# Running each token tile's load, first LayerNorm and transposes inside its own iteration in an eight-core S4 and LoRA kernel

## The chip, the cores and the metric

The kernel runs on all 8 cores of one Trainium2 chip. Each core takes 1024 of the 8192 tokens and computes its rows of the output alone; weights are read by every core. The metric is device time in microseconds (us) of the slowest core. Five engines work side by side on a core, each through its own list in order: PE (TensorE, matmuls and transposes), DVE (VectorE), ACT (ScalarE), POOL (GpSimd, here only to issue transfers) and SP (SyncE, which issues the other transfers).

## The reference, cut to what matters

```python
x = L0_attn_u                                   # (1, 8192, 4096) float32
x = x + _layernorm(_L0_attn_ref(_layernorm(x), ...))   # causal long convolution + D*u
x = x + _layernorm(_L0_ffn_ref(_layernorm(x), ...))    # x @ kernel + bias + LoRA terms

# _L0_attn_ref, along the last axis (L = 4096):
K = _s4_kernel(Lambda, p, q, B, Ct, step, L)
y = irfft(rfft(u, n=2*L) * rfft(K, n=2*L), n=2*L)[..., :L]
return y + D[0] * u

# _L0_ffn_ref, one LoRA choice per 1024 tokens:
base_out = x @ kernel + bias
Ax = einsum('bri,bti->btr', A_eff, x);  delta = einsum('bor,btr->bto', B_eff, Ax)
delta += einsum('or,btr->bto', lora_B_shared, einsum('ri,bti->btr', lora_A_shared, x))
return base_out + delta

# _layernorm(x): (x - mean) / sqrt(var + 1e-5), along the last axis
```

## The kernel before, in words

A core's 1024 tokens are 8 tiles of 128 tokens by 4096 features. The program has four stages. First a setup stage builds the convolution kernel as a banded matrix (`tband`) and the LoRA matrices. Then comes the tile loop, which the change touches: for every tile the first LayerNorm, the convolution, the second LayerNorm with its residual, the third LayerNorm and the transposed copy that the last matmuls need. Then the matmuls with the 4096 by 4096 weights run in 8 column blocks (L901), and at last the rows are read back, normalised and added (L951 to L972).

The order on each engine is the order in which the Python code emits instructions; there is no scheduler. Every instruction of DVE and ACT also waits for the one before it on its engine (L41). The work of one tile is in five functions:

- `emit_load_ln1` (L698): SP issues the load of the tile, 2 MB, into `xb[t % 2]` (L706). It waits until the tile two earlier, which held that buffer, has been stored and normalised. DVE sums the tile (L709) while ACT sums its squares (L713); DVE and ACT turn the sums into mean and scale in a chain of tiny operations (`ln_finalize`, L662 to L674); ACT writes the normalised tile in bf16 (L723) into `n1b` or `n1c`, which take turns.
- `emit_convtransp` (L726): PE transposes the 32 blocks of that tile into two PSUM buffers `ptrb` (L738), eight at a time; DVE copies each eight to `xfmt` (L742). There is one `xfmt`.
- `emit_conv` (L748): 8 groups of 4, 8, ..., 32 matmuls against `tband` (L763, 144 in all). Groups take turns on three PSUM buffers `pconv`, so the fourth group waits for the copy of the first. DVE adds `D` times the input as it copies a group out to `ya` (L770), ACT sums the squares (L775).
- `emit_post1` (L781): the second LayerNorm's statistics, the residual sum `x1` into `xb` (DVE, L794), its store to memory (SP, L798), and the third LayerNorm: sum (DVE, L801), squares (ACT, L806), small chain, normalised tile (ACT, L811) into the same bf16 buffer.
- `emit_post2` (L814): four rounds of eight transposes (PE, L823), a copy to `n2fm` (DVE, L827) and eight small matmuls with the LoRA matrix (PE, L834).

Before, the load and first LayerNorm of the next tile are emitted ahead of the convolution of the present one, and the next tile's transposes between `emit_post1` and `emit_post2` of the present one. After the last tile, DVE copies `pax` out (L855), and the column blocks start (L889).

Of the kernel before, what the change touches and what calls it, by code (L numbers as in the profile page):

```python
# [135 lines left out]
def build_nc(t_tiles=8):  # L136
    nc = bass.Bass("TRN2", target_bir_lowering=False)
    TT = t_tiles
# [37 lines left out]
    with ExitStack() as ctx:  # L176
# [482 lines left out]
        def ln_finalize(st, n_elems, t_s1tok, t_q1tok, a_guard=None):  # L659
            guards = [st.get("_ra"), a_guard]  # L660
            W("vector", [t_s1tok, t_q1tok] + [g for g in guards if g is not None])
            a = E("vector", lambda v: v.tensor_scalar(out=st["mean"][:, :], in0=st["s1"][:, :], scalar1=1.0 / n_elems, scalar2=None, op0=OP.mult))  # L662
            b = E("vector", lambda v: v.tensor_scalar(out=st["var"][:, :], in0=st["q1"][:, :], scalar1=1.0 / n_elems, scalar2=EPS, op0=OP.mult, op1=OP.add))
            W("vector", [a, b])
            c = E("vector", lambda v: v.tensor_scalar(out=st["rstd"][:, :], in0=st["mean"][:, :], scalar1=st["mean"][:, :], scalar2=-1.0, op0=OP.mult, op1=OP.mult))
            W("vector", [c])
            d = E("vector", lambda v: v.tensor_tensor(out=st["var"][:, :], in0=st["var"][:, :], in1=st["rstd"][:, :], op=OP.add))
            W("vector", [d])
            f = E("vector", lambda v: v.reciprocal(out=st["rstd"][:, :], in_=st["var"][:, :]))
            W("scalar", [f])  # L670
            g = E("scalar", lambda s: s.activation(out=st["rstd"][:, :], in_=st["rstd"][:, :], func=AF.Sqrt))
            st["_ra"] = g
            W("vector", [g])
            h = E("vector", lambda v: v.tensor_scalar(out=st["nbias"][:, :], in0=st["mean"][:, :], scalar1=st["rstd"][:, :], scalar2=-1.0, op0=OP.mult, op1=OP.mult))  # L674
            return g, h
# [22 lines left out]
        def emit_load_ln1(t_i):  # L698
            xbt = xb[t_i % 2]
            st = st1p[t_i % 2]  # L700
            nb = n1bufs[t_i % 2]
            war = [t_x1store[t_i - 2], t_n2_tok[t_i - 2], t_rs2_tok[t_i - 2]] if t_i >= 2 else (
                [t_ksum_done, t_bacc, t_bbcast] + xb0_guard if t_i == 0
                else [t_rdim, prev_ev] + xb1_guard + [t_ksum_done])
            W("sync", war)
            t_uload[t_i] = DMA("sync", f"uin{t_i % 2}", lambda s, t_i=t_i, xbt=xbt: s.dma_start(  # L706
                out=xbt[:, :], in_=u[P * t_i:P * t_i + P, :]))
            W("vector", [t_uload[t_i]] + (trv_guard if t_i == 0 else []))
            t_rs = E("vector", lambda v, xbt=xbt, st=st: v.tensor_scalar(  # L709
                out=trv[:, :], in0=xbt[:, :], scalar1=1.0, scalar2=None, op0=OP.mult, op1=OP.add,  # L710
                accum_out=st["s1"][:, :]))
            W("scalar", [t_uload[t_i]] + (tra_guard if t_i == 0 else []))
            t_sq = E("scalar", lambda s, xbt=xbt, st=st: s.activation(  # L713
                out=tra[:, :], in_=xbt[:, :], func=AF.Square, accum_out=st["q1"][:, :]))
            t_r1, t_nb1 = ln_finalize(st, D, t_rs, t_sq,
                                      a_guard=t_n1_tok[t_i - 2] if t_i >= 2 else None)
            toks = [t_nb1]
            if t_i >= 2:
                toks += [t_n2tr[t_i - 2], conv_ev_last[t_i - 2]]
            if t_i == 0:  # L720
                toks += [t_ldbs] + n1b_guard
            W("scalar", toks)
            t_n1_tok[t_i] = E("scalar", lambda s, xbt=xbt, st=st, nb=nb: s.activation(  # L723
                out=nb[:, :], in_=xbt[:, :], func=AF.Identity, bias=st["nbias"][:, :], scale=st["rstd"][:, :]))

        def emit_convtransp(t_i):  # L726
            nb = n1bufs[t_i % 2]
            evs = []
            for r in range(4):
                b = r % 2  # L730
                toks = [t_n1_tok[t_i], ptrb_last[b]]
                if t_i == 0 and r < 2:
                    toks += [t_astk, t_kmbT] + xfmt_guard
                W("tensor", toks)
                tlast = None
                for j in range(8):
                    c = 8 * r + j
                    tlast = E("tensor", lambda t, c=c, r=r, j=j, nb=nb: t.transpose(  # L738
                        out=ptrb[r % 2][:, 128 * j:128 * j + 128], in_=nb[:, 128 * c:128 * c + 128],
                        identity=idsb[:, :]))  # L740
                W("vector", [tlast] + (xfmt_guard if t_i == 0 and r == 0 else []))
                ev = E("vector", lambda v, r=r: v.tensor_copy(  # L742
                    out=xfmt[:, 1024 * r:1024 * r + 1024], in_=ptrb[r % 2][:, :]))
                ptrb_last[b] = ev
                evs.append(ev)
            ctr_ev[t_i] = evs

        def emit_conv(t_i):  # L748
            nb = n1bufs[t_i % 2]
            conv_ev = [None] * 8  # L750
            for g in range(8):
                toks = [ctr_ev[t_i][3], t_tband]
                if g >= 3:
                    toks.append(conv_ev[g - 3])
                elif t_i > 0:
                    toks.append(conv_ev_last[t_i - 1])
                else:
                    toks += [t_ksum_done, gb_toks[-1]]
                W("tensor", toks)
                tg = None  # L760
                for ij in range(4 * g + 4):
                    j0 = 512 * g - 128 * ij + 384
                    tg = E("tensor", lambda t, g=g, ij=ij, j0=j0: t.matmul(  # L763
                        out=pconv[g % 3][:, :], lhsT=xfmt[:, 128 * ij:128 * ij + 128],
                        rhs=tband[:, j0:j0 + 512], start=(ij == 0), stop=(ij == 4 * g + 3)))
                gw = []
                if g == 0:
                    gw = ([sqa_tok[t_i - 1]] if t_i >= 1 else []) + (ya_guard if t_i == 0 else [])
                W("vector", [tg] + gw)
                conv_ev[g] = E("vector", lambda v, g=g, nb=nb: v.scalar_tensor_tensor(  # L770
                    out=ya[:, 512 * g:512 * g + 512], in0=nb[:, 512 * g:512 * g + 512],
                    scalar=dbc[:, :], op0=OP.mult, in1=pconv[g % 3][:, :], op1=OP.add,
                    accum_out=yacols[:, g:g + 1]))
                W("scalar", [conv_ev[g]])
                E("scalar", lambda s, g=g: s.activation(  # L775
                    out=tra[:, 512 * g:512 * g + 512], in_=ya[:, 512 * g:512 * g + 512],
                    func=AF.Square, accum_out=yaqcols[:, g:g + 1]))
            conv_ev_last[t_i] = conv_ev[7]
            sqa_tok[t_i] = pr.now("scalar")
# [57 lines left out]
                        start=(c == 0), stop=(c == FC - 1)))  # L837
            t_n2tr[t_i] = last

        emit_load_ln1(0)  # L840
        emit_convtransp(0)
        for t_i in range(TT):
            if t_i + 1 < TT:
                emit_load_ln1(t_i + 1)
            emit_conv(t_i)
            emit_post1(t_i)
            if t_i + 1 < TT:
                emit_convtransp(t_i + 1)
            emit_post2(t_i)
        last_axmm = t_n2tr[TT - 1]  # L850
        last_convevac = conv_ev_last[TT - 1]
# [32 lines left out]
        for oc in range(8):  # L884
# [21 lines left out]
            for t2 in range(TT):  # L906
# [21 lines left out]
                if oc == 7:  # L928
                    t_i = t2
# [97 lines left out]
```

How the kernel before makes its waits and increments, by code:

```python
    def emit(self, en, fn):  # L37
        sem = self.esem[en]
        if en in ("vector", "scalar") and self.en_cnt[en] > 0:
            v = self.en_cnt[en]
            self.ops[en].append(lambda e, sem=sem, v=v: e.wait_ge(sem, v))
        self.en_cnt[en] += 1
        def wrapped(e, fn=fn, sem=sem):
            fn(e).then_inc(sem, 1)
        self.ops[en].append(wrapped)
        return (sem, self.en_cnt[en])
# [11 lines left out]
        def wrapped(e, fn=fn, sem=sem):  # L59
            fn(e).then_inc(sem, 16)
# [3 lines left out]
    def waits(self, en, toks):  # L64
        best = {}
        for t in toks:
            if t is None:
                continue
            sem, v = t
            k = id(sem)
            if k not in best or best[k][1] < v:
                best[k] = (sem, v)
        for sem, v in best.values():
            self.ops[en].append(lambda e, sem=sem, v=v: e.wait_ge(sem, v))
```

## Time and profile before

| | before |
|---|---|
| time, median of 3 runs | 1881.57 us (1880.63 to 1884.97) |
| the profiled execution, its own time | 1881.86 us |
| its span (slowest core, core 7) | 1880.3 us |
| spans of the eight cores | 1859.3 to 1880.3 us |
| busy PE / DVE / ACT / POOL | 938.4 / 438.6 / 309.7 / 167.4 us |
| tile loop, first convolution matmul to the end of the last tile | about 369 to 900 us |
| column blocks | about 901 to 1483 us |

Busy times are sums over the span, so they don't say what a stage waits for. In the tile loop each engine must be looked at inside one tile: which one works while the others wait, and what each waits for. All rows shown are of core 7. "Busy" of PE counts matmuls that overlap one another; how fast PE goes is read from the distance between starts.

### The profile page before, as it was taken

The page shows a single profiled execution, that of the slowest core. Times are in us where ns is not written, and L with a number is a line of the kernel's source. Part 1 is how long each engine was busy: PE and PEld are TensorE (multiplying, and loading weights), DVE is VectorE, ACT ScalarE, POOL GpSimd, SP SyncE. Part 2 cuts the span into 40 slices and gives each one's busy share as a digit, 9 for nine tenths or more (in the row PEclk, how much of TensorE's full clock was granted, in tenths as well). Part 3 has the DMA queues.
Part 4 walks back from the last instruction along what each step waited for, and adds up shares of the span by engine and source line. Part 5 has one row for each costly group of instructions (what it writes and reads, how often), then busy time and mean ns, then how long its engine had stood idle before and what let it go on. Part 6 is the DMA issues. An engine that isn't in the chain of part 4 may idle for free.

```text
span 1880.3 us, 13850 instructions; the slowest of 8 cores (1859.3 to 1880.3 us)
## 1 busy us (share of the span) xinstructions
PE 938.4 (50%) x4229; PEld 419.0 (22%) x4229; DVE 438.6 (23%) x826; ACT 309.7 (16%) x434; POOL 167.4 (9%) x313
## 2 busy tenths in 40 slices
PE   5350000268557756855889999999996000000000
PEld 1000000134333333432334334333433000000000
DVE  1232632343544454343010110011010111111111
ACT  2400000232323423322010110011010111111111
POOL 0002011000000000000123222222221000000000
PEclk9999999988678768867789899989988555555555
DMA  0001645311220221111556565556554333433433
GB/s 7 1 7 34 103 62 99 103 45 46 90 90 1 90 90 45 45 45 45 126 101 76 101 104 75 103 102 111 70 100 75 120 89 118 127 118 117 127 91 90
DMA packets 82715, 149.86 MB, mean 80 GB/s; under 512 B 18519, under 2 KB 51848, under 8 KB 78752
## 3 DMA queue, kind: packets, MB, share of 16 engines
q0 software_dynamic: 41248, 45.82, 18.7%
q1 hardware_dynamic: 41394, 103.15, 16.4%
q8 instruction: 35, 0.57, 0.1%
q14 instruction: 38, 0.31, 0.1%
HBM read 137.08 MB, written 52.23 MB: 101 GB/s over the span
## 4 chain that ended last, share of the span: by engine, by line
PE 45%; DMA 23%; DVE 15%; issue 6%; ACT 6%; SPq 2%; DVEq 1%; POOL 1%; ACTq 0%; POOLq 0%
PE pffn L901 24%; PE pconv L763 13%; DMA p3b<-f_scr 11%; DMA f_scr<-fstage 4%; ACT p3b L954 3%; DVE ya L964 3%; DVE xb L794 2%; DVE trv L801 2%; PE ptrb L823 2%; DMA trv<-lora_a 2%; PE pax L834 2%; DMA n1b<-lora_b 2%; DVE n2fm L827 1%; DMA wbuf<-wk 1%; SPq L968 1%
## 5 line engine op out<-in xcount | busy, mean ns | idle before, releaser
L901 PE MATMUL pffn<-wbuf,n2fm 128*128 128x512 bf16 x2048 | 463.9, 391 | 8.0 <-DMA wbuf<-wk 8.0
L763 PE MATMUL pconv<-tband,xfmt 128*128 128x512 bf16 x1152 | 264.6, 393 | 2.7 <-DVE ya L770 1.6
L901 PEld LDWEIGHTS pffn<-wbuf,n2fm 128*128 128x128 bf16 x2048 | 204.1, 100 | 267.8 <-issue 40.5
L896 POOL DMA_DIRECT2D wbuf<-wk x256 | 135.2, 529 | 965.7 <-PE pffn L901 955.9
L918 DVE TENSOR_SCALAR_CACHE_REDUCE fstage<-pffn 128x512 f32<-128x512 f32 x64 | 44.3, 691 | 502.1 <-PE pffn L907 485.7
L763 PEld LDWEIGHTS pconv<-tband,xfmt 128*128 128x128 bf16 x1152 | 115.1, 101 | 149.8 <-issue 24.9
L964 DVE SCALAR_TENSOR_TENSOR ya<-xb,nall,p3b 128x512 f32<-128x512 f32 x64 | 48.1, 751 | 352.2 <-ACT p3b L954 352.2
L922 ACT ACTIVATE tra<-fstage 128x512 bf16<-128x512 f32 x64 | 40.3, 629 | 528.2 <-DVE fstage L918 524.3
L954 ACT ACTIVATE p3b<-p3b,stf_nbias,stf_rstd 128x512 f32<-128x512 f32 x64 | 52.0, 813 | 343.5 <-DMA p3b<-f_scr 343.5
L738 PE MATMUL ptrb<-idsb,n1b 128*128 128x128 bf16 x128 | 12.5, 276 | 170.3 <-ACT n1b L723 118.8
L775 ACT ACTIVATE tra<-ya 128x512 bf16<-128x512 f32 x64 | 40.3, 629 | 176.5 <-DVE ya L770 173.7
L738 PEld LDWEIGHTS ptrb<-idsb,n1b 128*128 128x128 bf16 x128 | 11.0, 125 | 171.9 <-issue 171.1
L834 PE MATMUL pax<-n2fm,astkT 128*64 128x128 bf16 x256 | 33.0, 310 | 32.4 <-DVE n2fm L827 32.4
L713 ACT ACTIVATE tra<-xb 128x4096 bf16<-128x4096 f32 x8 | 28.9, 3617 | 110.0 <-DMA xb<-u 110.0
L770 DVE SCALAR_TENSOR_TENSOR ya<-n1c,dbc,pconv 128x512 f32<-128x512 bf16 x32 | 23.9, 747 | 95.8 <-PE pconv L763 76.4
L738 PE MATMUL ptrb<-idsb,n1c 128*128 128x128 bf16 x128 | 11.7, 264 | 67.2 <-DVE xfmt L742 67.2
L770 DVE SCALAR_TENSOR_TENSOR ya<-n1b,dbc,pconv 128x512 f32<-128x512 bf16 x32 | 23.9, 747 | 88.5 <-PE pconv L763 62.8
L889 PE MATMUL pffn<-bhl,ones2bs 2*128 2x512 bf16 x64 | 30.5, 498 | 26.9 <-DVE fstage L918 25.2
L709 DVE TENSOR_SCALAR_CACHE_REDUCE trv<-xb 128x4096 bf16<-128x4096 f32 x8 | 35.4, 4420 | 19.8 <-DMA xb<-u 19.0
L827 DVE COPY n2fm<-ptrb 128x1024 bf16<-128x1024 bf16 x32 | 22.1, 691 | 72.5 <-PE ptrb L823 72.5
L595 PE MATMUL ptrb<-idsb,trv 64*128 64x64 bf16 x32 | 2.3, 233 | 68.1 <-ACT trv L583 65.5
L806 ACT ACTIVATE tra<-xb 128x4096 bf16<-128x4096 f32 x8 | 28.9, 3617 | 43.9 <-DVE xb L794 43.9
(232 smaller groups left out, 636.9 us busy)
## 6 DMA issues: line engine op xcount, KB each, us to landing
wbuf<-wk POOLq DMA_DIRECT2D x256, 128.0 KB, 3.4
xb<-u SPq DMA_DIRECT2D x8, 2048.0 KB, 8.6
x_scr<-xb SPq DMA_DIRECT2D x8, 2048.0 KB, 6.3
xb<-x_scr SPq DMA_DIRECT2D x8, 2048.0 KB, 8.9
f_scr<-fstage SPq DMA_DIRECT2D x64, 256.0 KB, 2.7
p3b<-f_scr SPq DMA_DIRECT2D x64, 256.0 KB, 3.2
y<-ya SPq DMA_DIRECT2D x64, 256.0 KB, 2.3
n1b<-lora_b POOLq DMA_DIRECT2D x16, 256.0 KB, 4.2
```

What stands on the lines that cost most here:

```text
L763: tg = E("tensor", lambda t, g=g, ij=ij, j0=j0: t.matmul(out=pconv[g % 3][:, :], lhsT=xfmt[:, 128 * ij:128 * ij + 128], rhs=tband[:, j0:j0 ...
L770: conv_ev[g] = E("vector", lambda v, g=g, nb=nb: v.scalar_tensor_tensor(out=ya[:, 512 * g:512 * g + 512], in0=nb[:, 512 * g:512 * g + 512] ...
L775: E("scalar", lambda s, g=g: s.activation(out=tra[:, 512 * g:512 * g + 512], in_=ya[:, 512 * g:512 * g + 512], func=AF.Square, accum_out=y ...
L794: t_x1 = E("vector", lambda v, xbt=xbt: v.scalar_tensor_tensor(out=xbt[:, :], in0=ya[:, :], scalar=sta["rstd"][:, :], op0=OP.mult, in1=xbt ...
L827: t_ev2 = E("vector", lambda v, r=r, t_i=t_i: v.tensor_copy(out=bass.AP(n2fm, TOK * 8 * r + P * t_i, [[FC * TOK, P], [TOK, 8], [1, P]]), i ...
L834: last = E("tensor", lambda t, c=c, t_i=t_i: t.matmul(out=pax[:, P * t_i:P * t_i + P], lhsT=astkT[:, NS * c:NS * c + NS], rhs=bass.AP(n2fm ...
L896: t_wload[kg] = DMA("gpsimd", f"wload{kg % 4}", lambda g, f=f, oc=oc, kg=kg: g.dma_start(out=wbuf[kg % 4][:, :], in_=wk[128 * f:128 * f + ...
L901: tlast = E("tensor", lambda t, f=f, t2=t2, kg=kg: t.matmul(out=pffn[t2][:, :], lhsT=bass.AP(n2fm, TOK * f + P * t2, [[FC * TOK, P], [1, P]]),
L918: t_fev[(oc, t2)] = E("vector", lambda v, t2=t2, oc=oc, sbuf_i=sbuf_i: v.tensor_scalar(out=fstage[sbuf_i][:, :], in0=pffn[t2][:, :], scala ...
L922: t_fsq[idx] = E("scalar", lambda s, sbuf_i=sbuf_i, t2=t2, oc=oc: s.activation(out=tra[:, 512 * sbuf_i:512 * sbuf_i + 512], in_=fstage[sbu ...
L954: t_lnf = E("scalar", lambda s, fbuf=fbuf: s.activation(out=fbuf[:, :], in_=fbuf[:, :], func=AF.Identity, bias=stf["nbias"][:, :], scale=s ...
L964: p3_stt[i3] = E("vector", lambda v, t_i=t_i, pc=pc, fbuf=fbuf: v.scalar_tensor_tensor(out=ya[:, 512 * pc:512 * pc + 512], in0=xb[t_i % 2] ...
```

## The change

The prologue (load, LayerNorm and transposes of tile 0) goes, and so do the two guarded calls for tile `t_i + 1`. The loop calls all five functions for its own tile, in order. The functions themselves are the same, and so are the buffers: two `xb`, two bf16 tiles, one `xfmt`.

```diff
-        emit_load_ln1(0)
-        emit_convtransp(0)
         for t_i in range(TT):
-            if t_i + 1 < TT:
-                emit_load_ln1(t_i + 1)
+            emit_load_ln1(t_i)
+            emit_convtransp(t_i)
             emit_conv(t_i)
             emit_post1(t_i)
-            if t_i + 1 < TT:
-                emit_convtransp(t_i + 1)
             emit_post2(t_i)
```

On PE, from the first tile's transposes (`n1b`) to the second tile's convolution. Before:

```order
L738 MATMUL ptrb<-idsb,n1b 128x128 x32
L763 MATMUL pconv<-tband,xfmt 128x512 x144
L738 MATMUL ptrb<-idsb,n1c 128x128 x32
L823 MATMUL ptrb<-idsb,n1b 128x128 x8
L834 MATMUL pax<-n2fm,astkT 64x128 x8
```

Now, from the first tile's last round to the second tile's first:

```order
L823 MATMUL ptrb<-idsb,n1b 128x128 x8
L834 MATMUL pax<-n2fm,astkT 64x128 x8
L738 MATMUL ptrb<-idsb,n1c 128x128 x32
L763 MATMUL pconv<-tband,xfmt 128x512 x144
L823 MATMUL ptrb<-idsb,n1c 128x128 x8
```

The 32 transposes of the second tile (`n1c`) moved from in front of the four rounds of the first tile to behind them.

On DVE, from the third LayerNorm's last small operation of the first tile to the second tile's convolution. Before:

```order
L674 TENSOR_SCALAR st_nbias<-st_mean,st_rstd 128x1
L742 COPY xfmt<-ptrb 128x1024 x4
L827 COPY n2fm<-ptrb 128x8x128 x4
L709 TENSOR_SCALAR trv,st_s<-xb 128x4096
L662 TENSOR_SCALAR st_mean<-st_s 128x1
L663 TENSOR_SCALAR st_var<-st_q 128x1
L665 TENSOR_SCALAR st_rstd<-st_mean 128x1
L667 TENSOR_TENSOR st_var<-st_var,st_rstd 128x1
L669 RECIPROCAL st_rstd<-st_var 128x1
L674 TENSOR_SCALAR st_nbias<-st_mean,st_rstd 128x1
L770 SCALAR_TENSOR_TENSOR ya,yacols<-n1c,dbc,pconv 128x512 x8
```

Now:

```order
L827 COPY n2fm<-ptrb 128x8x128 [waits tok_tensor,tok_vector] x4
L709 TENSOR_SCALAR trv,st1b_s<-xb 128x4096 [waits dma_uin1,tok_vector]
L662 TENSOR_SCALAR st1b_mean<-st1b_s 128x1 [waits tok_vector,tok_scalar]
L663 TENSOR_SCALAR st1b_var<-st1b_q 128x1 [waits tok_vector]
L665 TENSOR_SCALAR st1b_rstd<-st1b_mean 128x1 [waits tok_vector]
L667 TENSOR_TENSOR st1b_var<-st1b_var,st1b_rstd 128x1 [waits tok_vector]
L669 RECIPROCAL st1b_rstd<-st1b_var 128x1 [waits tok_vector]
L674 TENSOR_SCALAR st1b_nbias<-st1b_mean,st1b_rstd 128x1 [waits tok_scalar,tok_vector]
L742 COPY xfmt<-ptrb 128x1024 [waits tok_tensor,tok_vector] x4
L770 SCALAR_TENSOR_TENSOR ya,yacols<-n1c,dbc,pconv 128x512 [waits tok_tensor,tok_scalar,tok_vector]
```

In both, a LayerNorm's sum and small chain (L709 to L674) stand between the copies of the last rounds and the second tile's convolution; before it is the third tile's, now the second tile's own. The four copies to `xfmt` moved behind it.

On SP, the first transfers of the loop, before (-) and now (+):

```order
 L657 DMA bhl<-bias_scr 2x4096
-L706 DMA xb<-u 128x4096 x2
+L706 DMA xb<-u 128x4096
 L798 DMA x_scr<-xb 128x4096
 L706 DMA xb<-u 128x4096
```

The second tile's load moved from right behind the first tile's load to right behind the store of the first tile's `x1`; every later load moves one tile back in the same way.

## Rows read from the trace of the kernel before

**Rows 1.** Windows (busy and count by engine, PE's granted clock, transfers): whole stages
```profile
core 7: us, PE busy (x) PEld busy (x) DVE busy (x) ACT busy (x) POOL busy (x), PEclk, DMA share, GB/s
567.00:633.00 66.00, 43.58 (x240) 23.13 (x240) 28.44 (x52) 21.28 (x26) 0.00 (x0) 0.76 0.16 64
900.00:1483.00 583.00, 508.07 (x2176) 215.80 (x2176) 47.22 (x132) 47.07 (x122) 133.00 (x252) 0.90 0.58 96
```
**Rows 2.** Windows, the same columns: inside the third and fourth tiles
```profile
501.40:535.00 33.60, 33.60 (x148) 14.80 (x148) 9.73 (x22) 9.36 (x18) 0.00 (x0) 0.93 0.00 1
535.00:555.80 20.80, 2.79 (x33) 2.35 (x31) 15.04 (x26) 8.64 (x7) 0.00 (x0) 0.63 0.24 101
555.80:567.90 12.10, 8.03 (x65) 6.42 (x66) 3.80 (x5) 3.51 (x1) 0.00 (x0) 0.50 0.44 173
```
**Rows 3.** Timeline (start, length, engine, line, idle before), end of the third tile
```profile
544.63 0.33 SPq L798 DMA_DIRECT2D x_scr<-xb  x1
551.78 3.80 ACT L811 ACTIVATE n1b<-xb,st_nbias,st_rstd 128x4096 bf16<-128x4096 f32 x1 [0.54 <-DVE st_nbias L674]
...
555.70 0.33 SPq L706 DMA_DIRECT2D xb<-u  x1
555.83 1.01 PE L823 MATMUL ptrb<-idsb,n1b 128*128 128x128 bf16 x8 [1.39 <-ACT n1b L811]
...
564.39 3.62 ACT L713 ACTIVATE tra<-xb 128x4096 bf16<-128x4096 f32 x1 [8.81 <-DMA xb<-u]
566.05 0.69 DVE L827 COPY n2fm<-ptrb 128x1024 bf16<-128x1024 bf16 x1 [2.32 <-PE ptrb L823]
566.86 4.42 DVE L709 TENSOR_SCALAR_CACHE_REDUCE trv<-xb 128x4096 bf16<-128x4096 f32 x1
567.85 32.96 PE L763 MATMUL pconv<-tband,xfmt 128*128 128x512 bf16 x144
571.54 0.15 DVE L662 TENSOR_SCALAR st_mean<-st_s 128x1 f32<-128x1 f32 x1 [0.24 <-DVE trv L709]
573.95 3.80 ACT L723 ACTIVATE n1b<-xb,st_nbias,st_rstd 128x4096 bf16<-128x4096 f32 x1 [0.59 <-PE pconv L763]
```
**Rows 4.** Timeline, first tile: from the loads to the convolution
```profile
335.37 1.14 SPq L706 DMA_DIRECT2D xb<-u  x2
351.08 4.42 DVE L709 TENSOR_SCALAR_CACHE_REDUCE trv<-xb 128x4096 bf16<-128x4096 f32 x1 [18.96 <-DMA xb<-u]
357.36 1.28 ACT L671 ACT_TABLE_LOAD   x1 [2.64 <-DVE st_rstd L669]
359.50 3.80 ACT L723 ACTIVATE n1b<-xb,st_nbias,st_rstd 128x4096 bf16<-128x4096 f32 x1 [0.65 <-DVE st_nbias L674]
363.55 1.87 PE L738 MATMUL ptrb<-idsb,n1b 128*128 128x128 bf16 x16 [118.77 <-ACT n1b L723]
368.98 7.39 PE L763 MATMUL pconv<-tband,xfmt 128*128 128x512 bf16 x24 [1.12 <-DVE xfmt L742]
```
**Rows 5.** Line L706 (loads), times to landing: the first two, then the other six
```profile
DMA to landing us min/median/max: 15.4/17.6/19.8
...
DMA to landing us min/median/max: 8.4/8.6/8.7
```
**Rows 6.** Lines L798 (stores of x1), then L896 (weights, the first four), times to landing
```profile
DMA to landing us min/median/max: 6.3/6.3/7.2
...
DMA to landing us min/median/max: 6.4/7.7/16.2
```
**Rows 7.** Waits of the tile loop: who, for whom, us, times, longest
```profile
PE pconv L763 <- DVE ya L770: 1.6, 4, 0.6
```
**Rows 8.** Timeline of PE's weight loads, one for each matmul: start of two convolutions
```profile
506.02 0.15 PEld L763 LDWEIGHTS pconv<-tband,xfmt 128*128 128x128 bf16 x1 [0.28 <-issue]
506.38 28.16 PEld L763 LDWEIGHTS pconv<-tband,xfmt 128*128 128x128 bf16 x131 [0.20 <-issue]
...
633.99 0.13 PEld L763 LDWEIGHTS pconv<-tband,xfmt 128*128 128x128 bf16 x2 [0.17 <-issue]
636.06 3.77 PEld L763 LDWEIGHTS pconv<-tband,xfmt 128*128 128x128 bf16 x18 [0.23 <-issue]
```

## The prediction
> **What bounds the kernel now.** I read the windows first, to see which stage the change touches. A tile takes 66 us of the loop and the column blocks behind it take 583 us [rows 1]; the change touches neither a matmul there nor a transfer of theirs, so I take those blocks and the last stage as shifted, not changed. Next the windows inside one tile [rows 2]: a convolution of 33.6 us in which PE is busy throughout; then 20.8 us in which PE has 2.8 us of work and DVE 15.0 (the post stage: statistics, `x1`, third LayerNorm); then 12.1 us of alternation of PE and DVE. That sum, 66.5, is the tile's period: the tile is a serial chain of convolution, LayerNorms and rounds. What the reader is to see is that the next tile's LayerNorm stands *beside* this chain, under the convolution.
>
> Then the timeline of one tile's end [rows 3]. The last copy of the rounds starts at 566.05, DVE goes to the sum of a following tile at 566.86, and PE starts the next convolution at 567.85, without waiting for that sum: its input was normalised and transposed before. The normalising pass of the tile prepared there runs at 573.95, when PE is six us into its convolution.
>
> **What the change puts on the chain.** After it, the convolution of tile t+1 needs the sum L709, the small chain, L723, 32 transposes and four copies, all emitted behind the rounds of tile t. Up to the last copy of the rounds nothing in front changes: the third LayerNorm's result ends at 551.78 + 3.80 = 555.58 and the first round starts at 555.83 [rows 3], and the `xfmt` copies that go from there ran beside L811, so their going gives nothing.
>
> From the sum's start the new chain is, in steady rows [rows 3]: L709 at 566.86 to L723 at 573.95, 7.09 us; L723 itself 3.80. Its last part was never on the chain later than tile 0, but there it was [rows 4]: L723 ends at 363.30, the transposes start at 363.55, and the convolution at 368.98, so 0.25 + 5.43 = 5.68 us. Sum 7.09 + 3.80 + 5.68 = 16.57. Tile 0 gives the same in one piece: 351.08 to 368.98 is 17.90, less its single table load of 1.28, 16.62 [rows 4]. Before, the same stretch (L709's start to the convolution's start) took 567.85 - 566.86 = 0.99 [rows 3]. So each of the 7 passages from a tile to the next costs 16.6 - 1.0 = **15.6 us, together 109.2**. Bounds for one passage: 15.0, if the transposes (1.87 us for 16 in rows 4) took half as long and only the copies counted; 17, if half a us of waiting came at each of three handovers.
>
> What lies beside other work: the load. SP now issues it right behind the store of `x1`: 544.63 + 0.33 = 544.96 on this time base, where before it waited until 555.70, since the buffer of the tile just finished had to be free [rows 3]. It is wanted at 566.86 by DVE, 21.9 us later. Alone a load lands in 8.4 to 8.7 us [rows 5] and a store in 6.3 [rows 6]; now they run together. The nearest rows for that are the two loads at 335.37, together 4 MB, which landed after 15.4 and 19.8 us [rows 5]. Even 19.8 is hidden. ACT's squares (3.62) come after landing and are wanted at 571.54: 544.96 + 19.8 + 3.62 = 568.4, hidden too. Cost 0; what is late next is DVE, which gets to L709 only after the four copies. Nothing else is queued behind the load on SP before the next store, a tile later. Without the cover, each us past 566.86 costs one us a tile.
>
> **What it gives back.** (1) DVE no longer has another tile's sum and chain in front of the first convolution copy. PE waited for these copies 1.6 us in the whole loop, 4 times [rows 7]; rounding up for waits that hide in the groups, -1.8. Bounds 0 and -4. (2) The first load no longer shares with the second. It landed in 15.4; alone the others take 8.6 [rows 5], but the first four weight loads run beside it and took 6.4 to 16.2 [rows 6]. So it lands in 8.6 to 15.4; I take 11, between, since the second load is the greater part of the other traffic: -4.5, bounds 0 and -6.8. The chain at that place is load, L709 and on [rows 4], so it counts in full.
>
> **The clock.** The matmuls at the start of every convolution are 0.43 us apart and later ones 0.22; the clock in the rounds ahead was 0.50, the 1.2 GHz level, and 0.93 over a convolution [rows 2]. The slow part lasted 5.0 us in the longest case (501.35 to 506.38) and 2.1 in the shortest (633.99 to 636.06) [rows 8]; half of its length is lost time. After the change PE has only transposes in the 10 us ahead of a convolution, as at tile 0. I add 0 for it. Bounds: each of 7 starts as the longest instead of the mean of the two, (5.0 - 3.55) / 2 x 7 = +5; each as the shortest, -5.
> The Trainium skill, "TensorE: Matmul & The Clock Gate", Part 4 (PE-mode transpose), says that transposes don't count as PE activity to the clock gate. Then every convolution would start as cold as the longest rows, and the sum would be 5 us higher; rows 2 can't tell, since real matmuls (L834) are mixed with transposes there and the clock is low all the same.
>
> **Sum.** 109.2 - 1.8 - 4.5 = +102.9. The profiled execution took 1881.86, so 1984.8; it lies 0.3 above the median of the runs, which leaves **1984.5 us**. Bounds together: passages 105 to 119, give-backs -10.8 to 0, clock -5 to +5. The ends don't meet all at once; 1972 to 1998 is the forecast's own range, with some us for the column blocks, whose weight loads meet other cores' traffic.
>
> **Rivals.**
>
> *The load comes too late.* Store and load in one queue, on all cores in step, might serialise worse than two loads. If the load took 19.8 only after the store's 6.3, it would land at 571.1, 4.2 late: 7 x 4.2 = +29, 2014. For it: the store is new beside the load. Against: the rows of two loads together have the same 4 MB and land inside the gap. Chance 0.04.
>
> *The load is exposed whole.* If the loop behaved as one without double buffering (the load starting when the tile's last work ends), 7 x 8.6 = +60 on top, 2045. The two `xb` are still there and SP's waits for tile t+1 are on tile t-1, so only a queue held by something unseen would do it. Chance 0.01. The Trainium skill, "Trainium Kernel Development and Optimization", Best Practices, tells to double-buffer so that DMA overlaps compute; read as a rule against this change it gives this case, yet what is given up here by the rows is the overlap of DVE, ACT and PE, not that of the load.
>
> *The clock stays down longer.* If all 24 matmuls of the first three groups ran at 0.43, a convolution would have 24 x 0.43 = 10.3 us of slow part instead of 3.55, 3.4 us lost, times 7 = +24, 2008. For it: PE idles longer ahead of a convolution. Against: at tile 0 PE had idled 118.77 us [rows 4] and its 24 matmuls took 7.39, not 10.3. Chance 0.04.
>
> *Not slower.* DVE has gaps of 2.32 us in each of four rounds (9.3 us) and ACT 8.81 [rows 3]. If the next tile's sum and chain ran in them and the transposes under L723, the passage would cost nothing and the give-backs stay: 1881.6 - 6.3 = 1875. It decides from the point where L709 starts before the first round's copy, near 557, which asks for 10 us sooner. Against: DVE takes its list in order, L709 stands behind the last L827, and L723 can't be read by PE before it ends. Chance 0.01.
>
> **How the numbers follow.** Forecast 0.90, the others 0.04, 0.01, 0.04, 0.01. About 0.2% (4 us) is what a measurement of this kernel can tell from no change. Faster has only the last rival, 0.01; within 0.2% is a sliver of the same kind, 0.01; slower 0.98. The range 1972 to 1998 leaves out the rivals (0.10) and some 0.08 of the forecast's tails.
>
> **What would show it.** In the profile after: periods of a tile near 82 us instead of 66; L709 directly behind the fourth L827, with no wait for the load; PE idle about 11 us between the last L834 and the first L738 and again in pieces to the convolution; the convolution itself 33 to 34 us as before, without waits for L770; `xb<-u` landing between 9 and 20 us, before DVE asks; the column blocks near 580 us. DVE idle before L709 with "DMA xb<-u" as its releaser would make the load the step that failed; a convolution of 36 us or more the clock; a column stage that differs by over 8 us would mean that I was wrong to take it as shifted.

## The result and the profile after

| | before | after |
|---|---|---|
| median | 1880.32 us (10 runs) | 1985.43 us (10 runs) |
| ratio after to before | | 1.0549, 95% interval 1.053 to 1.0568 |
| profiled execution, its span | 1881.86, 1880.3 us | 1985.44, 1983.1 us |
| first to last convolution start, the eight cores | 463.6 to 466.3 us | 566.6 to 568.9 us |

The plain medians are 105 us apart; the ratio, 1.0549, makes the cost 103 us. 1984.5 us, 102.9 more than before, had been predicted. A few executions of every kernel here are some per cent longer at a lower clock on one die; ratios leave them out, plain medians don't. Nearly all of the difference lies in the tile loop, which grew by 103.1 us on average over the cores. The slowest core of the profiled execution is now core 1; the rows of after are of that core. The lines behind the loop have moved up by four in the changed file (L901 is L897).

The windows of one tile, with the columns of [rows 1] (time, busy of each engine, PE's granted clock, transfers), answer to [rows 2]:

```profile
core 1: us, PE busy (x) PEld busy (x) DVE busy (x) ACT busy (x) POOL busy (x), PEclk, DMA share, GB/s
608.70:642.20 33.50, 33.50 (x144) 14.53 (x144) 5.29 (x14) 5.06 (x14) 0.00 (x0) 0.93 0.00 1
642.20:663.30 21.10, 0.03 (x1) 0.01 (x1) 12.28 (x22) 8.64 (x7) 0.00 (x0) 0.63 0.51 195
663.30:675.40 12.10, 8.03 (x64) 6.37 (x64) 3.45 (x5) 3.71 (x2) 0.00 (x0) 0.50 0.02 9
675.40:690.70 15.30, 3.75 (x33) 3.18 (x32) 7.57 (x12) 4.00 (x2) 0.00 (x0) 0.50 0.00 0
```

The first three stages are as long as before. A fourth one of 15.3 us is new, in which one engine at a time works. Where DVE had 9.73 us of work under the convolution it now has 5.29: what was hidden there came out. The timeline of the same tile's end (start, length, engine, line, idle before) answers to [rows 3, 4]:

```profile
652.11 0.33 SPq L798 DMA_DIRECT2D x_scr<-xb  x1
652.63 0.33 SPq L706 DMA_DIRECT2D xb<-u  x1
659.26 3.80 ACT L811 ACTIVATE n1c<-xb,st_nbias,st_rstd 128x4096 bf16<-128x4096 f32 x1 [0.54 <-DVE st_nbias L674]
664.95 3.62 ACT L713 ACTIVATE tra<-xb 128x4096 bf16<-128x4096 f32 x1 [1.89 <-DMA xb<-u]
673.55 0.69 DVE L827 COPY n2fm<-ptrb 128x1024 bf16<-128x1024 bf16 x1 [2.32 <-PE ptrb L823]
674.71 4.42 DVE L709 TENSOR_SCALAR_CACHE_REDUCE trv<-xb 128x4096 bf16<-128x4096 f32 x1 [0.47 <-DVE n2fm L827]
681.80 3.80 ACT L723 ACTIVATE n1b<-xb,st_nbias,st_rstd 128x4096 bf16<-128x4096 f32 x1 [0.59 <-DVE st_nbias L674]
685.85 1.87 PE L738 MATMUL ptrb<-idsb,n1b 128*128 128x128 bf16 x16 [10.43 <-ACT n1b L723]
690.76 10.59 PE L763 MATMUL pconv<-tband,xfmt 128*128 128x512 bf16 x38 [1.01 <-DVE xfmt L742]
```

DVE reaches L709 behind the last L827, and what ended its short idle was its own copy, not the load, whose data ACT had squared from 664.95 to 668.57. From that copy's start (673.55) to the convolution's (690.76) are 17.2 us; before, 1.80 (566.05 to 567.85, [rows 3]). Times to landing of the seven later loads, of the stores of `x1`, and of the first load:

```profile
DMA to landing us min/median/max: 11.8/12.2/14.5
...
DMA to landing us min/median/max: 6.3/7.1/9.2
...
DMA to landing us min/median/max: 13.7/13.7/13.7
```

In the waits of the loop the row of [rows 7], PE for L770, is gone. The rest of PE's waits ahead of a convolution is for the copies of the transposes:

```profile
PE pconv L763 <- DVE xfmt L742: 8.4, 8, 1.2
```

### The profile page after: what moved, and what is told of

It reads as the page before. It is cut to its first block, busy times and chain, and to the rows that moved or that the text cites. A ratio compares the mean times of both kernels' runs of the same rounds, so it can differ in the third digit from the quotient of the medians.

```text
span 1983.1 us, 13850 instructions; the slowest of 8 cores (1966.1 to 1983.1 us)
## 1 busy us (share of the span) xinstructions
PE 945.0 (48%) x4229; PEld 423.5 (21%) x4229; DVE 438.9 (22%) x826; ACT 309.7 (16%) x434; POOL 167.4 (8%) x313
## 4 chain that ended last, share of the span: by engine, by line
PE 44%; DMA 22%; DVE 16%; ACT 8%; issue 6%; SPq 2%; DVEq 1%; POOL 1%; ACTq 0%; POOLq 0%
PE pffn L897 23%; PE pconv L763 13%; DMA p3b<-f_scr 11%; DMA f_scr<-fstage 4%; ACT p3b L950 3%; DVE ya L960 2%; DVE xb L794 2%; DVE trv L801 2%; DVE trv L709 2%; PE ptrb L823 2%; DMA trv<-lora_a 2%; DMA n1b<-lora_b 1%; PE pax L834 1%; DVE n2fm L827 1%; PE ptrb L738 1%
## 5 line engine op out<-in xcount | busy, mean ns | idle before, releaser
L897 PE MATMUL pffn<-wbuf,n2fm 128*128 128x512 bf16 x2048 | 463.3, 390 | 4.9 <-DMA wbuf<-wk 4.9
L897 PEld LDWEIGHTS pffn<-wbuf,n2fm 128*128 128x128 bf16 x2048 | 204.1, 100 | 264.1 <-issue 36.8
L738 PE MATMUL ptrb<-idsb,n1b 128*128 128x128 bf16 x128 | 14.9, 309 | 147.4 <-ACT n1b L723 146.4
L823 PE MATMUL ptrb<-idsb,n1c 128*128 128x128 bf16 x128 | 16.5, 310 | 83.7 <-ACT n1c L811 83.7
L823 PE MATMUL ptrb<-idsb,n1b 128*128 128x128 bf16 x128 | 16.5, 310 | 83.6 <-ACT n1b L811 83.6
L770 DVE SCALAR_TENSOR_TENSOR ya<-n1b,dbc,pconv 128x512 f32<-128x512 bf16 x32 | 23.9, 747 | 113.1 <-PE pconv L763 113.1
L770 DVE SCALAR_TENSOR_TENSOR ya<-n1c,dbc,pconv 128x512 f32<-128x512 bf16 x32 | 23.9, 747 | 111.6 <-PE pconv L763 111.6
L738 PEld LDWEIGHTS ptrb<-idsb,n1b 128*128 128x128 bf16 x128 | 12.8, 142 | 149.4 <-issue 149.2
L827 DVE COPY n2fm<-ptrb 128x1024 bf16<-128x1024 bf16 x32 | 22.1, 692 | 99.2 <-PE ptrb L823 99.2
L885 PE MATMUL pffn<-bhl,ones2bs 2*128 2x512 bf16 x64 | 30.9, 505 | 26.3 <-DVE fstage L914 24.6
L713 ACT ACTIVATE tra<-xb 128x4096 bf16<-128x4096 f32 x8 | 28.9, 3617 | 72.7 <-DMA xb<-u 72.7
L709 DVE TENSOR_SCALAR_CACHE_REDUCE trv<-xb 128x4096 bf16<-128x4096 f32 x8 | 35.4, 4420 | 18.4 <-DMA xb<-u 17.2
L794 DVE SCALAR_TENSOR_TENSOR xb<-ya,sta_rstd,xb 128x4096 f32<-128x4096 f32 x8 | 35.9, 4484 | 0.8
```

Of the source, the lines that this page charges most:

```text
L794: t_x1 = E("vector", lambda v, xbt=xbt: v.scalar_tensor_tensor(out=xbt[:, :], in0=ya[:, :], scalar=sta["rstd"][:, :], op0=OP.mult, in1=xbt ...
L897: tlast = E("tensor", lambda t, f=f, t2=t2, kg=kg: t.matmul(out=pffn[t2][:, :], lhsT=bass.AP(n2fm, TOK * f + P * t2, [[FC * TOK, P], [1, P]]),
```

## The experiments

Theory: between a tile's last copy to `n2fm` and the next convolution stands a serial chain, each part costs what it measures, and the load is hidden. Rivals: the load, the clock, another engine. "Loop" is the time from the first to the last convolution start over the eight cores of the profiled execution: 464.6 us on average before, 567.7 after. All edits are to the changed kernel unless said. Where the load is split off, `emit_ln1` is `emit_load_ln1` without its L706.

**Transposes alone behind the rounds.**

```diff
+        emit_load_ln1(0)
         for t_i in range(TT):
-            emit_load_ln1(t_i)
             emit_convtransp(t_i)
+            if t_i + 1 < TT:
+                emit_load_ln1(t_i + 1)
             emit_conv(t_i)
```

> Only the 32 transposes and their copies stand behind the rounds of the tile ahead; load and LayerNorm of the next tile stay ahead of the convolution, as before. Theory (what counts is the serial chain between a tile's last copy to n2fm and the next convolution, and each part costs what it measures): the transposes start as soon as the last small matmul is done, so the passage is 1.8 + 4.9 = 6.7 us instead of 1.8, 7 times 5 = +35 on 1880, about 1915. Rival (only the LayerNorm makes the cost, the transposes hide): within 5 us of 1880. Rival (any prefetch that is broken costs the whole): about 1985.

1923.69 us, ratio 1.0232 (1.0204 to 1.0259). Loop 505 to 511, +42 where 35 was expected. The passage is right: 6.7 us from the last copy's start to the convolution in the trace. Neither rival holds. The other us a tile are a wait of PE for L770 that I had not priced here: 9.8 to 16.2 us in the loop by core, where the kernel before had 1.6 to 3.7. A timeline of core 0:

```profile
502.85 4.42 DVE L709 TENSOR_SCALAR_CACHE_REDUCE trv<-xb 128x4096 bf16<-128x4096 f32 x1
503.09 5.12 PE L763 MATMUL pconv<-tband,xfmt 128*128 128x512 bf16 x23 [1.23 <-DVE xfmt L742]
509.84 0.75 DVE L770 SCALAR_TENSOR_TENSOR ya<-n1b,dbc,pconv 128x512 f32<-128x512 bf16 x1
510.74 24.55 PE L763 MATMUL pconv<-tband,xfmt 128*128 128x512 bf16 x111 [2.53 <-DVE ya L770]
```

Here DVE starts the following tile's sum as the convolution starts, PE comes to it at full speed, fills its three buffers and waits 2.53 us. In the kernel before, the sum started a us ahead and every convolution started slowly, so this wait was only 1.6 us in all on core 7 [rows 3, 7].

**The load alone early.**

```diff
+        emit_load(0)
         for t_i in range(TT):
-            emit_load_ln1(t_i)
+            if t_i + 1 < TT:
+                emit_load(t_i + 1)
+            emit_ln1(t_i)
```

> The changed kernel, with the load of the next tile alone issued ahead of the convolution again (LayerNorm and transposes stay in their own iteration). Theory (the load was hidden in the changed kernel as well): no gain; the first load shares with the second again, so +1 to +3, 1985 to 1989. Rival (the late load or its company with the store holds DVE or ACT): 10 to 40 us faster than 1985.

Median 1990.93, ratio 1.0554 (1.0525 to 1.0584), beside 1.0549 for the changed kernel; loop 564.4 to 569.4. Giving the load all its time back gains nothing.

**A second store ahead of the load.**

```diff
+            DMA("sync", "x1out", lambda s, t_i=t_i, xbt=xbt: s.dma_start(
+                out=f_scr[P * t_i:P * t_i + P, :], in_=xbt[:, :]))
             t_x1store[t_i] = DMA("sync", "x1out", lambda s, t_i=t_i, xbt=xbt: s.dma_start(
```

> The changed kernel, with a second store of the same 2 MB in front of the store of x1 and so ahead of the next load. It measures the slack of the load. Theory: landing moves from 12.2 us after its issue to about 18.5, DVE wants it about 22 after: hidden, 1984 to 1989. Rival (the load was already near its limit): each us beyond costs 7 us, 2005 or more.

1985.14, ratio 1.0525 (1.0453 to 1.0596), loop 566.7 to 569.2. The loads land later, and nothing moves:

```profile
DMA to landing us min/median/max: 16.8/17.1/18.5
```

So some 5 us of slack at least were there. The load is out as a cause, from both sides.

**The sum cut to 8 columns.**

```diff
             t_rs = E("vector", lambda v, xbt=xbt, st=st: v.tensor_scalar(
-                out=trv[:, :], in0=xbt[:, :], ...
+                out=trv[:, 0:8], in0=xbt[:, 0:8], ...
```

> The changed kernel, with the first LayerNorm's sum taken over 8 of the 4096 columns (the rest of the sum is left out). Theory: DVE's sum of 4.42 us is on the chain in all 7 passages and becomes about 0.16; ACT's squares end long before, so 7 x 4.26 = -30, and about 1 us at the first tile, where the squares of 3.62 take over: about 1954. Rival (ACT's squares or the load are late next): the gain is cut to below 15, 1970 or more.

1942.36, ratio 1.0323 (1.0297 to 1.0349): 43 us gained, 31 expected; loop 526 to 533, 39 less. The chain shrank as expected: from L709 to L723 2.83 to 3.2 us instead of 7.1 to 7.5, 30 in 7 passages. Most of the rest is the clock: seven convolutions together took 9 us less on average over the cores. Windows around the transposes and the convolution's start, core 1, with PE's rows of the same stretch:

```profile
582.00:585.20 3.20, 0.04 (x1) 0.07 (x2) 0.00 (x0) 2.91 (x1) 0.00 (x0) 0.50 0.00 0
585.20:590.00 4.80, 3.58 (x32) 3.11 (x33) 2.77 (x4) 0.00 (x0) 0.00 (x0) 0.64 0.00 0
590.00:594.00 4.00, 3.99 (x19) 1.86 (x20) 1.51 (x4) 0.88 (x3) 0.00 (x0) 1.00 0.01 4
```

```profile
585.16 1.86 PE L738 MATMUL ptrb<-idsb,n1c 128*128 128x128 bf16 x16 [6.17 <-ACT n1c L723]
587.19 1.75 PE L738 MATMUL ptrb<-idsb,n1c 128*128 128x128 bf16 x16 [0.16 <-DVE xfmt L742]
```

The clock rose inside the transposes, and the convolution ran at the full 2.4 GHz from its first matmul. On this core all eight took 31.4 us, measured from the first matmul's start to the last L770's; in the changed kernel most took 33.4 to 33.7.

**PE kept busy in the gap: matmuls, then transposes.**

```diff
             emit_load_ln1(t_i)
+            for k in range(32):
+                if t_i > 0:
+                    E("tensor", lambda t: t.matmul(
+                        out=putil[:, :], lhsT=xfmt[:, 0:128], rhs=tband[:, 0:512],
+                        start=True, stop=True))
             emit_convtransp(t_i)
```

> The changed kernel, with 32 matmuls of 512 columns whose result nobody reads added on PE in the gap of 10.4 us between a tile's last small matmul and the next transposes. They take about 8.6 us (8 at 0.43, 24 at 0.216). Theory: the clock is low there because PE idles, and each convolution loses some 2 us to it; with the clock up, the convolution takes 31.4 instead of 33.5 and the transposes with copies 4 to 4.9: -14 to -21, 1964 to 1971. Rival (the clock's start is not set by what PE does in the gap, or it falls again before the convolution): 1985. Rival (the added work delays the transposes): slower than 1985.

1968.44, ratio 1.0455 (1.0419 to 1.0492), loop 552 to 555: 14 us less. Most convolutions took 31.4 us, transposes and copies 4.03 instead of 4.90. More work on PE made the kernel faster. The second form puts 80 transposes there instead (`ptrb[0]` from `tband`, after a wait for `ptrb_last[0]`):

```diff
+            if t_i > 0:
+                W("tensor", [ptrb_last[0]])
+                for k in range(80):
+                    E("tensor", lambda t: t.transpose(
+                        out=ptrb[0][:, 0:128], in_=tband[:, 0:128], identity=idsb[:, :]))
             emit_convtransp(t_i)
```

> The changed kernel, with 80 transposes whose result nobody reads added in the same gap in which the other experiment put 32 matmuls. They take 8.5 us at the low clock. Theory (the clock answers to transposes as it does to matmuls, as the clock that rose inside the second 16 transposes of one tile suggests): convolutions of 31.4 us and the transposes with copies 4.0, as with the matmuls: 1966 to 1972. Rival (the Trainium skill, TensorE: Matmul & The Clock Gate, Part 4: transposes don't count as activity): convolutions of 33.0 to 33.8 as in the changed kernel, 1985.

Median 2018.78, ratio 1.0558 (1.0518 to 1.0598), loop 567 to 569: no gain. That is the rival's number, but not for its reason. Windows of core 7, then PE's rows of the same stretch:

```profile
425.00:429.00 4.00, 2.99 (x28) 2.58 (x27) 2.89 (x2) 0.00 (x0) 0.00 (x0) 0.50 0.02 4
429.00:433.00 4.00, 4.00 (x60) 4.00 (x58) 2.91 (x6) 0.00 (x0) 0.00 (x0) 0.79 0.00 0
433.00:437.00 4.00, 0.79 (x15) 0.61 (x11) 0.38 (x2) 3.02 (x2) 0.00 (x0) 1.00 0.01 2
437.00:441.00 4.00, 2.60 (x24) 2.40 (x24) 1.38 (x2) 0.98 (x1) 0.00 (x0) 0.56 0.00 0
```

```profile
426.82 1.03 PE L834 MATMUL pax<-n2fm,astkT 128*64 128x128 bf16 x8 [1.01 <-DVE n2fm L827]
427.79 6.00 PE L845 MATMUL ptrb<-idsb,tband 128*128 128x128 bf16 x80
438.24 1.87 PE L738 MATMUL ptrb<-idsb,n1c 128*128 128x128 bf16 x16 [4.45 <-ACT n1c L723]
```

The clock was 0.50 when the 80 transposes began and 1.00 when they ended, with nothing but transposes on PE between. So they were done in 6 us instead of 8.5, 4.45 us of idle remained, and the clock fell again in it. The length of the idle alone doesn't decide how a convolution starts: behind 6.17 us of it, at the low clock, the kernel with the short sum started fast, and this one started slowly behind 4.45. What separates the two no run here shows. The next run has 150 instead of 80, and nothing else changed:

> As the run with 80 added transposes, but with 150. There the clock rose to its full level inside the 80, they were done after 6 us, and it fell again in the 4.5 us of idle behind them. With 150 the idle ahead of the next transposes is under 2 us. Theory (transposes lift and hold the clock, idle lets it fall): convolutions of 31.4 us in most tiles and a loop about 14 us shorter, 1968 to 1975. Rival (transposes lift it, but don't hold it): convolutions of 33 us and more, 1985.

1963.19, ratio 1.0427 (1.0407 to 1.0448), loop 551 to 554, with most convolutions at 31.4 us. PE's rows at one passage, core 3:

```profile
666.46 9.49 PE L845 MATMUL ptrb<-idsb,tband 128*128 128x128 bf16 x150
676.96 1.05 PE L738 MATMUL ptrb<-idsb,n1b 128*128 128x128 bf16 x16 [1.01 <-ACT n1b L723]
...
680.99 31.24 PE L763 MATMUL pconv<-tband,xfmt 128*128 128x512 bf16 x144 [1.01 <-DVE xfmt L742]
```

Transposes lift the clock and, with an idle of 1.01 us left behind them instead of 4.45, it holds until the convolution.

**The LayerNorm between the third LayerNorm and the rounds.** Load early as above, and:

```diff
             emit_post1(t_i)
+            if t_i + 1 < TT:
+                emit_ln1(t_i + 1)
             emit_post2(t_i)
```

> The changed kernel, with the next tile's load issued ahead of the convolution and its LayerNorm emitted between the third LayerNorm and the four rounds; the transposes stay behind the rounds. This is the rival 'not slower' made real in part: sum and chain run while ACT normalises, and L723 under the rounds. Theory: the first copy to n2fm waits for the chain, 1.4 us later than now; then rounds as now, 1.8 for the last matmuls, 4.9 for the transposes: a passage 9 us shorter than in the changed kernel, 7 x 9 = -63, about 1922, which is some 40 above the kernel before. Rival (DVE's sum moved in front of the rounds costs there what it saves behind them): about 1985.

1946.19, ratio 1.0304 (1.0245 to 1.0363); loop 522 to 527, 43 less, not 63. The rival is refuted, my size too. Rows of core 7 (`emit_ln1` has moved lines: L714 is the sum, L718 the squares, L816 the third LayerNorm's result, L728 the first's, L832 the copy):

```profile
640.83 4.42 DVE L714 TENSOR_SCALAR_CACHE_REDUCE trv<-xb 128x4096 bf16<-128x4096 f32 x1
640.85 3.80 ACT L816 ACTIVATE n1c<-xb,st_nbias,st_rstd 128x4096 bf16<-128x4096 f32 x1 [0.54 <-DVE st_nbias L674]
644.75 3.62 ACT L718 ACTIVATE tra<-xb 128x4096 bf16<-128x4096 f32 x1
...
651.29 0.69 DVE L832 COPY n2fm<-ptrb 128x1024 bf16<-128x1024 bf16 x1
651.40 3.80 ACT L728 ACTIVATE n1b<-xb,st_nbias,st_rstd 128x4096 bf16<-128x4096 f32 x1 [0.59 <-DVE st_nbias L674]
```

The sum is done at 645.2, but the squares stand behind L816 on ACT and end at 648.4; the chain and the rounds' first copy wait for them. That is 3.1 us a tile, 22 in all, that I had left out. In all the rounds' last copy comes 5.0 us later behind its convolution than in the changed kernel, where 1.4 had been expected; some 5 us over the loop came back because more convolutions started fast.

**The first weight loads behind the first load.**

```diff
-                W("gpsimd", war)
+                W("gpsimd", war if kg else [t_uload[0]])
```

> The changed kernel, with the first four weight loads issued only once the first tile has landed. In the changed kernel the first load took 13.7 us with these four beside it, where 11 had been forecast; in the kernel before it took 15.4 with them and the second load. Theory (the weight loads, not the second load, were what the first load shared with): it lands in 8.4 to 9 us, the first convolution starts 5 us sooner, the weights are still there long before they are used: about 1980. Rival (it is slow for another reason, such as the cores asking at once or memory being turned from the setup's writes): still 12 to 14 us, 1985.

The first load of the slowest core lands in 8.3 us instead of 13.7; over the eight cores it takes 7.8 to 8.3 instead of 10.7 to 13.7:

```profile
DMA to landing us min/median/max: 8.3/8.3/8.3
```

From the issue of `bhl` to the first convolution the cores take 26.3 to 27.1 us instead of 29.2 to 32.2, 3.9 us on average. The ratio is 1.0524 (1.0506 to 1.0542) against 1.0549 (1.053 to 1.0568): in that direction, but the intervals overlap, and the absolute 1986.59 stood beside a kernel before of 1888.18. From the first matmul behind the loop (L885) to the end the cores took 976 to 987 us here, 972 to 982 in the changed kernel, which no run explains. The cause of the landing time is shown by the trace; the gain in the total is not settled.

**The other way: more overlap instead of less.** The four rounds of a tile go between the groups of the next convolution, the next transposes right behind the convolution, and the next LayerNorm behind group 6 (groups counted from 1; `g` in the code counts from 0). The third LayerNorm writes to `trv` instead of the bf16 tile, and the sums' unused outputs go to the bf16 tile instead of `trv`.

```diff
# in emit_conv, behind the matmuls of group g
+                if t_i > 0:
+                    if g >= 4:
+                        emit_p2_mm(t_i - 1, g - 4, p2_ev)
+                    if 3 <= g <= 6:
+                        p2_tr = emit_p2_transp(t_i - 1, g - 3)
# behind the copy of group g
+                if t_i > 0 and 3 <= g <= 6:
+                    p2_ev = emit_p2_copy(t_i - 1, g - 3, p2_tr)
+                if g == 5 and t_i + 1 < TT:
+                    emit_ln1(t_i + 1)
# the loop, behind load 0, load 1, LayerNorm 0 and transposes 0
         for t_i in range(TT):
             emit_conv(t_i)
+            if t_i + 1 < TT:
+                emit_convtransp(t_i + 1)
             emit_post1(t_i)
+            if t_i + 2 < TT:
+                emit_load(t_i + 2)
```

> Opposite direction to the change: the four rounds of a tile go between the groups of the next convolution, the next transposes stand right behind the convolution, the next LayerNorm behind its sixth copy, and the third LayerNorm's result goes to a buffer of its own. PE then has a convolution's first three groups to do during the LayerNorms. Theory of the serial chain: from a convolution's last copy: 4.9 transposes and copies, 4.9 statistics, 9.2 residual and sum, 2.4 chain, then 120 matmuls 26 and rounds 5: a period of about 52 instead of 66, 7 x 14 = -98, about 1785. Rival (the rounds between groups and the waits of DVE give the time back inside the convolution): within 20 us of 1880.

1792.16, ratio 0.9499 (0.944 to 0.9558); loop 352 to 353, periods of 52 to 53.5 us behind the first. The last tile, which the loop as measured here leaves out, is some 15 us longer, since its convolution too holds rounds and a wait. The version beats both kernels. The waits of its loop, core 3 (L782 is the convolution's copy there), name what is late next:

```profile
PE pconv L770 <- DVE ya L782: 75.4, 7, 10.9
```

The last run takes that wait: the third LayerNorm's sum and chain go behind the first three copies of the next convolution, the rounds two at a time behind groups 6 and 7, the next LayerNorm behind group 7.

```diff
# behind the copy of group g, emit_post1b being emit_post1 from L801 on
+                if g == 2 and t_i > 0:
+                    emit_post1b(t_i - 1)
+                    if t_i + 1 < TT:
+                        emit_load(t_i + 1)
```

> The version with the rounds inside the convolution, further: the third LayerNorm's sum and chain stand behind the first three copies of the next convolution instead of ahead of them, the rounds go two at a time behind groups 6 and 7, and the next LayerNorm behind group 7. There PE waited 10.9 us a tile for those copies. Theory: PE goes on 7.5 us sooner; then the chain over x1, third LayerNorm, load (8.6), first LayerNorm and transposes is next, about 46 us a tile instead of 53: 1745 to 1760. Rival (the load, which now starts when the third LayerNorm is done, takes the whole gain): 1785 or more.

**1757.59, ratio 0.9362 (0.9314 to 0.941)**; loop 333 to 338, periods of 48 to 50 us behind the first, where 46 had been expected. This is the fastest version, by the ratio 120 us below the kernel before. Rows of core 7 (L707 load, L837 third LayerNorm's result, L852 copies of the rounds, L715 sum, L744 transposes), and the times to landing of its loads from there on:

```profile
426.37 3.80 ACT L837 ACTIVATE trv<-xb,st_nbias,st_rstd 128x4096 bf16<-128x4096 f32 x1 [0.54 <-DVE st_nbias L674]
430.30 0.33 SPq L707 DMA_DIRECT2D xb<-u  x1
...
440.60 1.49 DVE L852 COPY n2fm<-ptrb 128x1024 bf16<-128x1024 bf16 x2 [0.81 <-PE ptrb L845]
...
442.21 4.42 DVE L715 TENSOR_SCALAR_CACHE_REDUCE n1b<-xb 128x4096 bf16<-128x4096 f32 x1
...
453.30 1.86 PE L744 MATMUL ptrb<-idsb,n1b 128*128 128x128 bf16 x16 [4.52 <-ACT n1b L729]
...
DMA to landing us min/median/max: 8.1/8.2/8.7
```

SP issues the load only once the third LayerNorm's result of the tile two earlier is out, and PE idles 4.5 us for the LayerNorm behind it. But the load is not what comes last: it landed at 438.96, 8.7 us after its issue, and in the later tiles too 2 to 4 us before DVE's sum. The sum stands behind the rounds' last copies on DVE's list (440.60), and these wait for PE's transposes. So the load, which the expectation had in the chain, had slack. By these rows a next version would have to move the sum in DVE's list, and a third `xb` alone would gain little; neither was tried.

## Why the prediction was right

Point by point, by its own steps:

- **A passage costs 15.6 us.** Measured from the last L827's start to the convolution: 17.05 on average on core 1 (16.8 to 17.2) instead of 1.80, so 15.25, 107 in all where 109.2 was said. Over the eight cores it is 106.5. Two errors cancel in part: L709 to L723 took 7.09 to 7.46 us, 7.23 on average, where 7.09 had been taken; the transposes and copies took 4.90 instead of the 5.43 of tile 0. In tile 0 of the kernel after they took 5.42 again, so the first time is the odd one, and a first execution of a stretch was a poor model for the later ones. Cutting the sum, moving the transposes alone and moving the LayerNorm each moved the loop as parts of this chain.
- **The load costs 0.** Shown from both sides: earlier gains nothing, a second store ahead of it costs nothing. With the store it lands in 12.2 us, less than the 15.4 and 19.8 of the two loads used as a bound, which had the four weight loads beside them.
- **DVE's relief gives 1.8.** The wait of PE for L770 is gone, and the convolutions, first matmul to last copy, went from 33.41 on average (core 7 before, seven tiles) to 33.16 (core 1 after) and 33.02 (core 7 after): 1.8 to 2.7 over the loop. But core 7, whose 1.6 us were the source of the term, waited least: over the eight cores the waits came to 1.6 to 3.7 us, 2.4 on average, and the seven convolutions became 3.2 us shorter. The term was too small. With the passages that gives 106.5 - 3.2 = 103.3 for the loop, which grew by 103.1.
- **The first load gives 4.5.** This term was mis-sized. The stretch from `bhl` to the first convolution became 0.9 us shorter on average over the cores (31.4 to 30.6). The load landed in 13.7, where 11 had been taken as nearer to a load alone. And the 15.4 that it was to be subtracted from was the latest of eight: before, the first load took 10.5 to 15.4 us, 12.8 on average, and after 10.7 to 13.7, 11.9 on average. The step that failed is "the second load is the greater part of the other traffic": the four weight loads were what delayed the first load, as the run that issues them later shows, with 8.3. The value was inside the bounds named.
- **The clock gives 0.** Right as a difference: the seven convolutions together have 60 matmul starts about 0.43 us apart before and 59 after, on average over the cores. They are spread otherwise, though: before, every convolution starts slowly; after, most do (33.3 to 33.8 us) and one or two a core don't (31.4). That the two sums agree is luck: nothing in the prediction says why they should. The experiments show that some 2 us a tile lie there, 14 to 15 us over the loop with the gap filled. The rule of the Trainium skill that was weighed (TensorE: Matmul & The Clock Gate, Part 4, that transposes don't count as activity) is not borne out here: with transposes alone the clock rose from 0.50 to 1.00, and behind 150 of them it held.
- **The column blocks are shifted only.** From the first L885 or L889 to the end: 968 to 980 us on the cores before, 972 to 982 after, so any difference there is less than their spread.

The mechanism, a serial passage with a hidden load, is shown. That the total was met to within 1 us is in part luck. The cost was put 2.7 us too high by the passages (109.2 for 106.5) and 1.4 too high by the waits (1.8 given back for 3.2); it was put 3.6 too low by the first load (4.5 given back for 0.9) and about 1 too low by the stages behind the loop, for which there was no term. These cancel.

The rivals fell as weighed. The one with an exposed load, for which the Trainium skill's advice to double-buffer ("Trainium Kernel Development and Optimization", Best Practices) had been cited, would have cost 60 us; the buffers are still two, and what the change gave up was overlap between engines. "Not slower" asked for the LayerNorm ahead of the rounds; placed there by hand it takes back 43 of the loop's 103 us, and to take more the order had to be opened further.

## What to carry to other kernels

Where each engine runs its list in order, a hidden step costs nothing until it is written behind something; then it costs its own length, chain and handovers included, and the price can be read from the first iteration, where it was never hidden, less what happens only the first time. Ask for the load apart from the arithmetic: with two buffers its issue moved, but it had 22 us until it was wanted and took 12. And read the chain the other way too: the same rows that priced the loss showed PE busy for 44 of 66 us a tile [rows 1], and that was worth 120 us.

## What the runs showed of the hardware

- PE's granted clock rose from 0.50 to 1.00 under 80 transposes alone and fell again over the idle of 4.45 us behind them; behind 150 it held over an idle of 1.01 us and through 32 further transposes.
- 32 matmuls or 150 transposes that nobody reads, in a gap of 10.4 us, made the whole kernel 0.9% and 1.2% faster (ratios 1.0455 and 1.0427 against 1.0549).
- A 2 MB load issued 0.5 us behind a 2 MB store lands in 12.2 us, alone in 8.4 to 8.7 [rows 5], behind two stores in 17.1. Four weight loads of 128 KB each as written, from float32 in memory, made the first load take 10.7 to 13.7 by core; without them it took 7.8 to 8.3.
